# First attention of a four-stage kernel: the loads of queries and keys in another order on SyncE's queue

## The reference

```
# first attention (4 heads of 32 channels), x after a folded batch norm
qkv = einsum('oc,bchw->bohw', pw_w, x);  q, k, v = split(...)
attn = softmax(einsum('bnchw,bncyx->bnhwyx', q, k) / sqrt(32), axis=-1)
x = einsum('oc,bchw->bohw', out_w, einsum('bnhwyx,bncyx->bnchw', attn, v)) + out_b + input
# then on tokens: a causal attention with 64 heads of 2 channels, and a gated sum of 8 expert networks
t = t + _L1_attn_ref(_ln_t(t), ...)
t = t + _L1_ffn_ref(_ln_t(t), ...)
```

## Time and profile before

| | |
|---|---|
| median of 3 runs | 3389.75 us (3385.29 to 3397.03) |
| profiled execution, own time | 3398.41 us |
| its span, first to last instruction | 3396.7 us |
| mean granted TensorE clock | 0.974 |
| PE busy | 3078.5 us (91%) |
| DVE busy | 2062.5 us (61%) |
| ACT busy | 2711.0 us (80%) |
| first attention | 75 to some 860 us |

### The profile page before, as it was taken

The page is one execution under the profiler, slowest core; times in us unless marked ns, Lnnn a source line. Parts: engine busy times, 40 slices in busy tenths (PEclk is TensorE's granted clock), DMA queues, the critical chain, the costliest instruction groups (busy, mean ns, idle before and its releaser), DMA issues.

```text
span 3396.7 us, 70341 instructions
## 1 busy us (share of the span) xinstructions
PE 3078.5 (91%) x27633; PEld 1087.3 (32%) x27633; DVE 2062.5 (61%) x2974; ACT 2711.0 (80%) x2580; POOL 263.9 (8%) x350
## 2 busy tenths in 40 slices
PE   6899999999798898998999899899998988999999
PEld 3444444444322222222222222222222222233444
DVE  4788878888656456556556556656656643443333
ACT  5444444445499999999999999999999999973555
POOL 6000000000110011011010110101101000000000
PEclk9899999999899999999999999999999999998999
DMA  6121211120100110210210210210210211001000
GB/s 224 53 53 44 53 47 34 44 52 20 53 16 18 59 26 18 61 27 17 59 29 18 59 27 20 59 27 17 60 29 18 59 27 37 19 15 63 13 12 12
DMA packets 132542, 135.73 MB, mean 40 GB/s; under 512 B 27414, under 2 KB 111476, under 8 KB 132220
## 3 DMA queue, kind: packets, MB, share of 16 engines
q1 hardware_dynamic: 131216, 130.44, 13.9%
q10 hardware_dynamic: 1004, 0.83, 0.1%
HBM read 70.31 MB, written 51.41 MB: 36 GB/s over the span
## 4 chain that ended last, share of the span: by engine, by line
ACT 39%; PE 35%; issue 19%; DVE 5%; DMA 1%; SPq 1%; ACTq 0%; POOL 0%; DVEq 0%
ACT arena L961 38%; PE ps L1318 5%; PE ps L1371 3%; PE ps L1040 3%; PE ps L1365 3%; PE ps L1087 3%; PE ps L1406 3%; PE ps L1114 3%; PE ps L1089 3%; PE ps L1098 2%; PE ps L1069 2%; PE ps L1270 2%; DVE arena L1480 1%; DVE arena L1487 1%; DVE arena L1492 1%
## 5 line engine op out<-in xcount | busy, mean ns | idle before, releaser
L961 ACT ACTIVATE arena<-ps 128x1536 f32<-128x1536 f32 x1536 | 2068.3, 1636 | 21.6 <-PE ps L1270 21.2
L1318 PE MATMUL ps<-arena 128*32 128x512 f32 (+3 forms) x12288 | 1257.8, 504 | 1.9 <-DVE arena L1755 1.7
L1755 DVE TENSOR_TENSOR arena<-arena,causal 128x512 f32<-128x512 f32 x1024 | 664.5, 688 | 314.1 <-ACT arena L961 304.6
L1270 PE MATMUL ps<-arena 15*128 15x512 bf16 (+3 forms) x6144 | 606.9, 331 | 160.7 <-ACT arena L961 151.1
L890 ACT ACTIVATE arena<-ps 128x512 f32<-128x512 f32 x512 | 299.8, 596 | 278.8 <-PE ps L1089 268.2
L1270 PEld LDWEIGHTS ps<-arena 15*128 15x128 bf16 x6144 | 163.0, 92 | 1100.6 <-ACT arena L961 958.7
L1318 PEld LDWEIGHTS ps<-arena 128*32 128x32 f32 x12288 | 284.7, 109 | 385.1 <-issue 331.4
L1480 DVE TENSOR_REDUCE arena<-ps 128x32 bf16<-128x1024 f32 x256 | 311.2, 1216 | 119.9 <-PE ps L1069 119.9
L1487 DVE TENSOR_TENSOR arena<-arena,ps 128x512 f32<-128x512 f32 x512 | 329.2, 680 | 33.5 <-PE ps L1098 32.6
L1740 DVE COPY arena<-ps 128x512 f32<-128x512 f32 x256 | 176.5, 690 | 219.9 <-PE ps L1318 218.9
L1087 PE MATMUL ps<-arena 96*128 96x256 bf16 x1024 | 260.7, 279 | 0.3 <-ACT arena L863 0.2
(11 more groups left out here) (200 smaller groups left out, 1970.9 us busy)
## 6 DMA issues: line engine op xcount, KB each, us to landing
arena<-qstack SPq DMA_DIRECT2D x512, 30.0 KB
parts<-arena SPq DMA_DIRECT2D x8, 1536.0 KB, 6.3
arena<-parts SPq DMA_DIRECT2D x48, 256.0 KB, 5.4
arena<-parts SPq DMA_DIRECT2D x96, 128.0 KB, 2.8
arena<-kstack SPq DMA_DIRECT2D x512, 24.0 KB
qstack<-arena SPq DMA_DIRECT2D x24, 384.0 KB, 3.3
attn<-arena SPq DMA_DIRECT2D x512, 12.0 KB
arena<-arena SPq DMA_DIRECT2D x384, 16.0 KB, 1.8
```

Of the source, the lines that this page charges most:

```text
L961: act.activation(PR1[:, at:at + CW], bank(BPC * (f % 2), BPC), ACT.Exp).then_inc(d_exp, 1)
L1270: mm = pe.matmul(bank(at + k)[:, s * P:(s + n) * P], Ks[par][HR * h:HR * h + QROWS, j * P:(j + 1) * P], Qs[par][HR * h:HR * h + QROWS, t * ...
L1318: mm = pe.matmul(o[HR * h:HR * (h + 1), :], V1[n % 2][:, j, v:v + HR], pr[:, h * HALF + s * P:h * HALF + (s + k) * P], start=not opened[hi ...
L1755: dve.tensor_tensor(v, v, m3, ALU.min).then_inc(d_mask, 1)
```

## The change

Only `feed` changes. The low queries of the next image are issued ahead of the `RS` loads of step 1 instead of behind them. The keys leave the place behind the `RS` loads of step 3; they are issued behind those of step 0 of the next image (a quarter of an image later), ahead of the values. Waits, sizes and numbers of transfers stay the same.

```diff
             def feed(i, last=False):
                 for st in range(2 * STEPS):
                     g = i * (2 * STEPS) + st
+                    par, q = st // STEPS, st % STEPS
+                    b, sub = i * 2 + par, i * TURN + par * (TURN // 2)
+                    if not (last and par == 1) and q == 1:
+
+                        sp.wait_ge(b_qk, sub * 2 + 2 * SUB * (STEPS // 2))
+                        load_q(b + 1, 0)
                     for r, part_made in enumerate((b_rhi, b_rmid, b_rlo)):
...
-                    par, q = st // STEPS, st % STEPS
-                    b, sub = i * 2 + par, i * TURN + par * (TURN // 2)
-                    if not (last and par == 1) and q in (1, 2):
-
-                        sp.wait_ge(b_qk, sub * 2 + 2 * SUB * (STEPS // 2) * q)
-                        load_q(b + 1, q - 1)
-                    if not last and q == 3:
+                    if not (last and par == 1) and q == 2:
+
                         sp.wait_ge(b_qk, sub * 2 + TURN)
-                        load_k(b + 2, par)
+                        load_q(b + 1, 1)
                     first_image = isinstance(i, int) and i == 0 and par == 0
                     if q == 0 and not first_image and not (last and par == 1):
 
+                        sp.wait_ge(b_qk, sub * 2)
+                        load_k(b + 1, 1 - par)
                         sp.wait_ge(b_pv, sub)
                         load_v(b + 1, 1 - par)
```

## The result

| | before | changed |
|---|---|---|
| median, 9 runs each | 3388.63 us | 3378.47 us |
| ratio | | 0.9974, 95% interval 0.9961 to 0.9986 |
| median in a second comparison (29 and 12 runs) | 3385.73 us | 3378.83 us |
| ratio there | | 0.9983, interval 0.9973 to 0.9993 |
| profiled execution, own time | 3398.41 us | 3380.33 us |

The changed kernel is faster by 7 to 10 us, 0.2 to 0.3%. The profiled executions differ by 18, and why they say more than the runs is the main thing to learn here.

The account below looks back on a forecast made before the run. PE sets the pace, DVE close behind, and stalls for low queries at image starts. Gains of 4.43 (images 1, 2, 7) and 8.02 us (3, 5) give 12.45, rounded 12.5, off the median 3389.75: 3377 us, range 3369 to 3388.

Parts of the forecast that it names:

- The five waits: PE's waits for low queries at L1069, starts of images 1, 2, 3, 5, 7: go whole; gain bounds 8.0 and 12.45 us.
- rival 3: At L1069, DVE's maxima or ACT's guard, late for the same reason, hold it as long: 3390 us; chance 0.07.
- The half clock behind images 3 and 5: Lowered PE clock behind these two starts' waits goes with them: 8.02 us gained there, 3.58 if it stays.
- rival 1: At images 3 and 5 the waits go, the half clock does not: 8.0 us gained, 3382 us; chance 0.20.
- the 0.3% to which I gave 0.32: Whole kernel: time within about 0.3% (10.2 us) of before, what a measurement can tell from no change; chance 0.32.
- Taking the gain from the median: Whole kernel: the profiled execution's gain taken unchanged from the runs' median, 3389.75 - 12.5 = 3377.2 us.
- Images 4 and 6: Starts where the loop jumps back: PE stands 3.78 and 3.83 us ahead of L1055, hiding the query load; costed at 0.
- Keys, values and queries as one train: 2.88 MB between step 0's and step 1's `RS` loads, 14.5 us at 198 GB/s, ending about 237.8: cost 0.
- The slack of 0.6 us at step 0's `RS` loads: Last `RS` load lands at 223.5, PE uses it at 224.10, keys' packets right behind: taken as 0, bound 1.2 us.

Follow-up runs that it names:

- k_only: Against the kernel before, only the keys moved a quarter image later, low queries left behind the `RS` loads of step 1: 3386.19 us, ratio 1.0003.
- after_again: The changed kernel run once more against the kernel before: 3378.83 us against 3385.73, ratio 0.9983.
- q_only: Against the kernel before, only the low queries moved in front, keys left behind the `RS` loads of step 3: 3378.76 us, ratio 0.9979.
- one_train: The changed kernel with keys and values issued behind the low queries, as one train of 2.88 MB: 3375.43 us, ratio 0.9970 to the kernel before.
- late_queries: The kernel before with the low queries held longer (wait for 46 instead of 32 score groups), so every start waits longer: 3418.75 us, ratio 1.0095.
- unroll_before: The kernel before, loads in the old order, with the first attention's loop written out on TensorE, VectorE and ScalarE: 3377.92 us, ratio 0.9975.

## Why the prediction was right, and where it was not

- **Which loads are waited for, and where.** Right. The five waits went, whole, and nothing took their place (rival 3 fell): the low queries alone give the gain, the keys alone nothing.
- **Their size.** 8.0 us of waits by the timeline of before; the mean gain over the runs is 7.7 to 7.8. The 12.9 us that the prediction quotes for five places are image 0's 6.9 and the waits of images 2, 3, 5 and 7; its sum did not use them.
- **The half clock behind images 3 and 5.** This term, 4.4 us, was mis-sized. It was there in the one execution I read, and it went in the profile after, so that the stage shows 15.3 us of gain. But in `k_only` the same waits, 1.44 and 1.80 us, kept the clock at 1.00, and over 29 and 21 runs the mean clock did not rise. With a mean gain of 7.8 us, give or take 2, the waits' 8.0 leave this term 0 to some 2 us in the mean, which is rival 1 (3382 by its sum). Of the measured gains by the medians, 10.2 us lies between that rival's 8.0 and the forecast's 12.5, and 6.9 below both. The range 3369 to 3388 holds the time. The gain in the first comparison, 0.26%, lies within the 0.3% to which I gave 0.32.
- **The time itself.** That 3377 lies within 2 us of the measured 3378.5 and 3378.8 is in part luck: a gain forecast too large was taken from a median of three runs, 3389.75, which stands 3 us above the mean of all runs of before, 3386.4.
- **Taking the gain from the median.** I noted that the profiled execution lay 8.7 us above the median and yet took its gain unchanged. Such an execution is long because its clock was low (0.974), and a term made of clock is just what it overstates.
- **Images 4 and 6.** Their wait was hidden by the jump: shown, since with the loop written out the same order waits 1.85 and 1.37 us there. They came out at 1.78 and 0.93 us less than before, which I had costed at 0 with a bound of 5.6; the pauses became 0.3 and 0.9 us shorter, and half clock went from 13.7 to 10.2 us behind image 4's and stayed at 10.2 behind image 6's. Both vary by as much where the low queries stand in front as well (pauses of 3.39 and 3.52 us in `after_again`, 13.7 us of half clock behind image 6's in `q_only`), so it is not shown that the change gains anything there.
- **The jump is an engine's own cost.** Shown by writing it out on PE, then on the other two: 11 us, then another 6 by the medians (4 to 5 by the means; the intervals of these two versions overlap, so the second step rests on the profile, where the 1.28 and 1.01 us are gone). The Trainium skill ("Runtime: NRT & Kernel Launch", Instruction fetch mechanics) says that a taken branch to a target outside the fetched pages forces a fetch before execution goes on; the runs agree in that the pause goes with the branch and stays with ScalarE's while ScalarE has one. What fills the pause no run here shows.
- **Keys, values and queries as one train.** Cost 0, as said, even when `one_train` begins it 9.2 us ahead of the `RS` loads in place of 15.8. The slack of 0.6 us at step 0's `RS` loads held: `RS` made PE wait once for 2.0 us, in image 0, as in the earlier trace rows.

## What to carry to other kernels

A wait of 1 to 2 us on the engine that sets the pace was worth about its own length here (7.8 us for 8.0 of waits, and 15 for 11.1 in the version with the loop written out); count what the clock loses behind it only if several executions show it, and compare each run's clock before taking a gain from one profile. When the wait is for a load, look at what stands ahead of the load in its queue and issue it as soon as its buffer is free: nothing but the order had to change. Look for pauses labelled "issue" that repeat at a loop's jump: here they cost more than the late loads, and hid two waits for them.

## What had not been expected of the hardware

- A stall of some 4 us of PE (at images 4 and 6 two of 2.1 to 3.5 us close behind each other) was followed by 10 to 14 us near 1.2 GHz at all seven starts of `late_queries`, one under 2 us by none in most cases, and by 3.4 to 10 us in three of the 17 read closely (5 each in `before` and `k_only`, 7 in `unroll_before`).
- A loop's jump over a long body costs PE 2.7 to 3.9 us, and ScalarE's alone still 1.0 to 1.3 us of PE's time. Writing out three engines' loops made a 3379 us kernel 14 to 18 us faster, and the longer program left no idle time of PE over 0.8 us from 130 to 829 us.
- 222 GB/s of loads did not slow PE or VectorE: the row maxima took 1208 ns with and without them, the exact scores 274 and 275.
